# Scan runs of a four-layer kernel: four of the 64 products by C of each run go to VectorE, and the products with D's diagonal are set one by one

## The reference

```python
def step(hst, inp):
    dt_t, B_t, C_t, x_t = inp
    dA = jnp.exp(dt_t[:, :, None] * A)
    hst = hst * dA + (dt_t * x_t)[:, :, None] * B_t[:, None, :]
    y = jnp.einsum('bds,bs->bd', hst, C_t)
    return (hst, y)
...
y = jnp.transpose(ys, (1, 0, 2)) + xm * D_param
```

## Time and profile before

| what | us |
|---|---|
| median of 3 runs | 1950.43 (1948.98 to 1952.22) |
| span of the profiled execution, first to last instruction | 1947.4 |
| what lies around the span (1950.43 less 1947.4; the page gives no time of its own for the profiled execution) | 3.0 |
| the six runs from their first scan to their last, together | 938.0 |
| TensorE busy over the span | 1845.8 (95%) |
| VectorE, ScalarE, GpSimd busy | 1602.8, 1424.0, 1049.0 |

### The profile page before, as it was taken

How to read it: one execution, slowest core, us unless ns; L and a number is a source line. 1 busy time by engine, 2 the same in 40 slices (tenths; PEclk the granted TensorE clock), 3 DMA queues, 4 the chain that set the end, 5 groups by cost and what they waited for, 6 DMA issues and landing times.

```text
span 1947.4 us, 32682 instructions
## 1 busy us (share of the span) xinstructions
PE 1845.8 (95%) x12312; PEld 1335.2 (69%) x12312; DVE 1602.8 (82%) x2125; ACT 1424.0 (73%) x2661; POOL 1049.0 (54%) x603
## 2 busy tenths in 40 slices
PE   6989899998999999999999999999998999999997
PEld 3664899848998599969995899689974333332323
DVE  5565799678998699989995999889977999999742
ACT  3426899468993899799974999799954377777775
POOL 3031599526994299939980699479944400003000
PEclk9989899998999999999999999999998799999999
DMA  5022111111111112101110111021101111111000
GB/s 202 1 85 99 61 55 61 44 64 33 56 60 37 52 51 60 51 24 55 56 44 2 44 55 56 24 75 57 56 15 33 37 42 37 37 36 36 18 23 22
DMA packets 57547, 95.18 MB, mean 49 GB/s; under 512 B 14951, under 2 KB 23559, under 8 KB 55982
## 3 DMA queue, kind: packets, MB, share of 16 engines
q1 hardware_dynamic: 55854, 88.90, 14.9%
q0 software_dynamic: 1536, 4.20, 0.7%
HBM read 73.55 MB, written 6.91 MB: 41 GB/s over the span
## 4 chain that ended last, share of the span: by engine, by line
PE 66%; POOL 9%; ACT 9%; DVE 8%; issue 6%; DMA 1%; SPq 1%; DVEq 0%; ACTq 0%; POOLq 0%
PE PS L865 12%; PE PS L840 11%; POOL A L1019 8%; PE PS L256 7%; PE PS L1603 6%; PE PS L1556 6%; PE PS L846 5%; PE PS L1763 5%; PE PS L265 3%; DVE A L1569 2%; PE PS L872 2%; ACT A L931 2%; PE PS L441 2%; ACT A L908 1%; DVE ST L206 1%
## 5 line engine op out<-in xcount | busy, mean ns | idle before, releaser
L1019 POOL TENSOR_TENSOR A<-A 128x1024 f32<-128x1024 f32 x384 | 897.7, 2392 | 228.7 <-ACT small L923 104.4
L931 ACT ACTIVATE A<-A,negA 128x512 f32<-128x512 f32 x768 | 546.7, 714 | 30.8 <-DVE A L1000 24.1
L1000 DVE TENSOR_TENSOR_SCAN A<-A,PS 128x512 f32<-128x512 f32 x384 | 435.8, 1200 | 46.6 <-PE PS L846 24.1
L1000 DVE TENSOR_TENSOR_SCAN A<-A,small,PS 128x512 f32<-128x512 f32 x384 | 453.9, 1258 | 8.0 <-ACT A L931 5.0
L865 PE MATMUL PS<-ident,A 128*128 128x128 f32 x3072 | 409.1, 276 | 21.5 <-ACT A L737 13.1
L840 PE MATMUL PS<-A 128*128 128x128 f32 x3072 | 384.2, 276 | 1.5 <-ACT A L915 1.2
L865 PEld LDWEIGHTS PS<-ident,A 128*128 128x128 f32 x3072 | 352.9, 143 | 31.2 <-ACT A L737 15.6
L840 PEld LDWEIGHTS PS<-A 128*128 128x128 f32 x3072 | 363.2, 192 | 4.3 <-DVE A L1000 2.8
L1569 DVE TENSOR_REDUCE A<-PS 128x1 f32<-128x512 f32 x512 | 319.5, 681 | 40.2 <-PE PS L1556 38.7
L1800 ACT ACTIVATE A<-PS 128x512 f32<-128x512 f32 x512 | 267.4, 602 | 102.1 <-PE PS L1763 101.9
L908 ACT ACTIVATE A<-A,small 128x512 f32<-128x512 f32 x320 | 228.3, 714 | 21.7 <-PE PS L846 21.3
(11 more groups left out here) (194 smaller groups left out, 1802.5 us busy)
## 6 DMA issues: line engine op xcount, KB each, us to landing
A<-scrc SPq DMA_DIRECT2D x192, 256.0 KB, 3.1
A<-A SPq DMA_DIRECT2D x360, 32.0 KB
scr<-A SPq DMA_DIRECT2D x4, 1024.0 KB, 4.8
W<-in_wa SPq DMA_DIRECT2D x2, 1536.0 KB, 9.7
X<-in_x SPq DMA_DIRECT2D x4, 512.0 KB, 5.5
scr<-W SPq DMA_DIRECT2D x128, 1.5 KB
out<-X SPq DMA_DIRECT2D x4, 512.0 KB, 2.9
W<-in_w SPq DMA_DIRECT2D x1, 1984.0 KB, 7.7
```

The costliest lines, as they stand in the source:

```text
L931: e.activation(A_B[i % 4], r.DT[:, dt, ci * 512:(ci + 1) * 512], ACT.Exp, scale=negA[:, r.n, dt * 16 + s:dt * 16 + s + 1]).then_inc(*decay ...
L1000: e.tensor_tensor_scan(h, a, u, init, ALU.mult, ALU.add).then_inc(*scanned.up((q, i)))
L1019: e.tensor_tensor(h, h, CB[k % 2].unsqueeze(1).broadcast_to([128, 2, 512]), ALU.mult).then_inc(*weighed.up((q, pair)))
```

## The change

Three things change. Pairs 15, 31, 47 and 63 are multiplied by C's row on VectorE instead of GpSimd, each behind the scans of the next pair (before the scan of unit 34, 66 and 98, and behind the last scan), with a semaphore of its own. TensorE, ScalarE and SyncE do what they did, and wait for that semaphore where it is one of these pairs. The products with D's diagonal, four in a row at units 19, 23, 27 and 31 of each half, stand one at a time behind each odd unit from k = 3 to k = 10 of the half.

```diff
+        ON_VECTOR = (15, 31, 47, 63)
+
+        def weighed_at(q, pair):
+            return (weighed_v if pair in ON_VECTOR else weighed).at((q, pair))
...
                 if k >= 2:
-                    w.wait_ge(*weighed.at((q, 2 * (k - 2) + 1)))
+                    w.wait_ge(*weighed_at(q, 2 * (k - 2)))
+                    w.wait_ge(*weighed_at(q, 2 * (k - 2) + 1))
...
-                w.wait_ge(*weighed.at((q, pair)))
+                w.wait_ge(*weighed_at(q, pair))
...
-            def add_skip(ci, dt):
+            def add_skip(ci, n):
+                dt, j = divmod(n, 4)
                 w.wait_ge(*dve.at(("diag", q)))
-                for j in range(4):
-                    e.matmul(PS[:, j, dt * 128:(dt + 1) * 128], r.U[:, dt, ci * 512 + j * 128:ci * 512 + (j + 1) * 128], diag[:, dt, :],
-                             start=open_y(ci, j), stop=True, skip_group_check=True)
+                e.matmul(PS[:, j, dt * 128:(dt + 1) * 128], r.U[:, dt, ci * 512 + j * 128:ci * 512 + (j + 1) * 128], diag[:, dt, :],
+                         start=open_y(ci, j), stop=True, skip_group_check=True)
...
-                if dt == 3 and 4 <= s < 8:
-                    add_skip(ci, s - 4)
+                if 3 <= s < 11 and dt % 2:
+                    add_skip(ci, 2 * (s - 3) + dt // 2)
...
+            def weigh(pair):
+                k = pair // 2
+                w.wait_ge(*scanned.at((q, 2 * pair + 1)))
+                if r.steps[k][0] == r.order[0]:
+                    w.wait_ge(*carried.at((q, pair)))
+                w.wait_ge(*transfer(f"c_load{k % 2}").at((q, k)))
+                h = r.H[pair % HS]
+                e.tensor_tensor(h, h, CB[k % 2].unsqueeze(1).broadcast_to([128, 2, 512]), ALU.mult).then_inc(*weighed_v.up((q, pair)))
+
             for i in range(UNITS):
                 k, dt = divmod(i, 4)
                 ci, s = r.steps[k]
+                if i % 2 == 0 and i // 2 - 2 in ON_VECTOR:
+                    weigh(i // 2 - 2)
...
+            weigh(PAIRS_N - 1)
...
             for pair in range(PAIRS_N):
+                if pair in ON_VECTOR:
+                    continue
```

More of the change, by code:

```diff
@@ L159, in program @@
         decayed, scanned, carried = sig("decayed"), sig("scanned"), sig("carried")
-        weighed, added = sig("weighed_by_c"), sig("added_up")
+        weighed, weighed_v, added = sig("weighed_by_c"), sig("weighed_by_c_on_vector"), sig("added_up")
         taken = sig("y_taken")
```

## The result

The changed kernel took 1956.36 us (median of 7 runs, 1953.58 to 1961.40), the kernel before 1950.43 (1948.29 to 1952.22): ratio 1.0029, 95% interval 1.0017 to 1.0041. Slower, by 5.9 us between the medians: a small difference, 0.3%, but the interval lies wholly above 1. The forecast was slower, 1957.8 us.

The account below looks back on a forecast made before the run. TensorE was taken to bound each run until scan 72, then VectorE's queue, GpSimd 0.2 us behind. Terms 1.4 + 3.0 + 3.0 = 7.4 us gave 1954.8, plus 3.0 (median above span) 1957.8; own range 1954 to 1962, wider 1946 to 1970.

Parts of the forecast that it names:

- What bounds the kernel: In each run: TensorE's queue sets scan 72, VectorE's own queue sets the end from there, GpSimd 0.2 us late.
- D's products, taken 0 for scan 72: First half: spreading them shrinks VectorE's waits, but TensorE has the same records, so scan 72 doesn't move; 0 us.
- Products 15 and 31: Before scan 72: 1.14 us each, covered by VectorE's idle time in runs 0, 1, 2, 4; 31 costs +1.14 in runs 3, 5.
- The extra 0.6 us a run: At product 31: if GpSimd is no earlier, VectorE waits 0.6 us for pair 30, 3.6 over six runs.
- Product 47: After scan 72: +1.14 us in each run, less 0.8 of recovered waits for TensorE, net +0.34.
- Pair 62 late by 0.95 us: End of a run: GpSimd's product ends 0.95 us behind the last scan, not 0.2; +0.75 in four runs, 3.0 in all.
- Waiting products: Rival at 31 and 47: VectorE's products wait for GpSimd's, 1.93 us each, 23 us and 1981, or 1972; chance 0.15.
- Idle time goes: Rival: VectorE's idle 4.2 us a run goes and 3.4 comes, -4.6 us in all, 1945.8; chance 0.13.
- Nearly all covered: Rival: all 1.1 us of waiting comes back and pair 62 isn't late, 2.5 us, 1952.9; chance 0.20.

Follow-up runs that it names:

- e10: Kernel before with D's products of the first half left out and those of the second spread, no product by C on VectorE; ratio to before 0.9902.
- e2: Kernel before with only D's products spread in both halves, all products by C on GpSimd; ratio to before 0.9975.
- e3: Changed kernel with product 47 given back to GpSimd, 15, 31 and 63 staying on VectorE; ratio to before 0.9998.
- e4: Changed kernel with two more products, 39 and 55, on VectorE, six in all; ratio to before 1.0089.
- e7: Changed kernel with only product 47 on VectorE, D's products spread in both halves; ratio to before 1.0009.
- e13: Kernel before with D's products spread in the second half alone, no product by C on VectorE, nothing left out; ratio to before 1.0016.
- e1: Changed kernel with D's products in groups as before, products 15, 31, 47 and 63 still on VectorE; ratio to before 1.0040.
- e5: Changed kernel with VectorE's products 15, 31 and 47 set one scan later; ratio to before 1.0095.
- e12: As e10, D's products of the first half left out, but with products 15 and 63 on VectorE; ratio to before 0.9919.
- e11: Changed kernel with D's products of the first half left out, 15, 31, 47 and 63 on VectorE; ratio to before 0.9960.
- e8: Changed kernel with only product 31 on VectorE, D's products spread in both halves; ratio to before 0.9992.

## Why the prediction was right, and where it wasn't

**What bounds the kernel.** TensorE until scan 72: right, by e10 and by the scan 72 that e2 leaves unmoved. VectorE from there: right, by the 1.13 us per product in e3, e4 and e7. That GpSimd stands 0.2 us beside it: right (pair 62 ends 0.12 to 0.30 us behind the last scan), and more important than I made it (e13).

**D's products, taken 0 for scan 72.** Right: from scan 14 to scan 72 of run 0 69.68 us before, after and in e2. That the place of these records in the first half earns nothing was too narrow; it sets when GpSimd can start its catching up, and how much pause is left behind product 15.

**Products 15 and 31.** Covered in runs 0, 1 and 2, as said (in run 4 scan 72 came 0.24 us later, with the slower start of that run: its first 14 scans took 18.1 us instead of 16.8); in runs 3 and 5 scan 72 came 1.04 us later behind scan 14, for a reckoned 1.14. The cover was reckoned too simply: the idle 2.57 us of the stretch were counted wherever they lay, and most of them lay ahead of product 15. It held because the spread moved them (e1 shows the case without). The extra 0.6 us a run that I named for a GpSimd no earlier didn't come with the change (the 24 products take 1.19 to 1.32 us); it shows in e1, where product 31 takes 0.44 us more in run 0.

**Product 47.** 1.14 less 0.8, +0.34; seen: from scan 14 to the end of the last scan +0.18, +0.18, +0.19 and +0.42 us in runs 0, 1, 2, 4. The recovered waits were 0.96, not 0.8. Runs 3 and 5, reckoned +1.5: +1.55 and +1.30, 0.26 of the former in a second half at a granted clock of 0.98. This half of the sum was reckoned at 4.4 us and is 3.8 by the trace.

**Pair 62 late by 0.95 us, 3.0 us in all: wrong.** It ends 0.10 to 0.12 us behind the last scan, and the gating begins 0.15 us sooner behind it in runs 0 and 1, at the same distance in 3 and 5. The failing step is "GpSimd starts about 1.1 us late. At 2.33 against 2.34 it doesn't make that up". I put VectorE's product into GpSimd's queue as a delay, and not into the scans that GpSimd runs after: they are later by the same 1.14 us. The rows of pair 48 and 49 show both, 3.26 us and then a wait of 0.22 for VectorE.

**The sum.** By the trace the stretches with the changed instructions cost 3.5 us, not 7.4. The measured 5.7 has 2.2 more. All three lie inside the interval of 3.3 to 8.0, so the measured time alone doesn't tell them apart; the rest of the changed kernel's span is 6.5 us longer than before's, and a part of the 2.2 may lie there. That 1957.8 came within 1.5 us of 1956.36 owes something to luck: a term of 3.0 that isn't there stands beside about 2 us that the moved instructions don't explain.

**The rivals.** Waiting products: hardly with the change (at most 0.12 us, product 31 of run 1), but one scan later they cost 12.9 us, and without the spread a first part of it is seen. Idle time goes: VectorE's idle time between scan 14 and pair 31 did shrink, 2.57 to 1.41 us, and only because products filled it; refuted by e2, which leaves scan 72 in place. Nearly all covered: its 2.5 us was nearer to the traced 3.5 than the forecast's 7.4 was; of its two reasons one was right, that pair 62 isn't late, and the other nearly, 0.96 of the 1.1 us of waiting came back. So the mechanism by the traces is this rival's rather than the forecast's, though the measured 5.7 is nearer to 7.4 than to 2.5.

The better version is the spread with all products on GpSimd (e2), 1945.0 us, or with 15 and 63 moved (e6), 1944.9: both faster than the kernel before and the changed one (ratios 0.9975 and 0.9972). They don't differ measurably.

## What to carry to other kernels

Where three engines are busy for the same time, cut a run at the places where another engine begins to set the pace, and price an edit in each piece by the rule of that piece: here the same product cost nothing before scan 72 in the runs where TensorE set the pace there, and 1.13 us behind it. When an inserted instruction delays a producer, the consumer's deadline moves with it. Before moving work between VectorE and GpSimd with both operands in SBUF, see where the other one stands at that moment; a relief can turn into a wait for the very work that is left (e5, e12).

## What was not expected of the hardware

Stretches without any changed instruction differ between the profiled executions. The first scan starts between 202.6 us (e1) and 209.0 (e7, e12), and from the last scan of run 5 to the end it takes 521.6 us (e1) to 526.0 (e13). The window from 80 to 130 us, of before and then of the changed kernel, columns as above:

```profile
80.00:130.00 50.00, 48.39 (x349) 44.12 (x348) 32.41 (x117) 17.18 (x30) 4.92 (x3) 0.97 0.17 61
```

```profile
80.00:130.00 50.00, 48.28 (x320) 43.43 (x319) 29.20 (x109) 17.31 (x30) 4.92 (x3) 0.90 0.12 42
```

TensorE is busy for the same 48 us and gets through 349 or 320 records, with a mean granted clock of 0.97 or 0.90, a mixture of its levels of 2.4 and 1.2 GHz; in the 80 us ahead of it it had been busy for 62.1 and 61.7 us. In before, e4, e5, e6, e10 and e11 the first scan starts at 205.2 to 205.5 us, at a clock of 0.97 in this window (e1 too, 202.6); in the others at 208.2 to 209.0, at 0.90 or 0.93. The same at the start of a run: the first 14 scans of run 2 take 18.17 us in before at a granted clock of 0.91, and 16.78 in e1 at 1.00. And inside a run: in run 3 of e8 the way from scan 72 to the last is 1.1 us longer than in its other runs, with 0.97 in a window where they have 1.00. One profile per kernel doesn't show whether this goes with a kernel or an execution. The table gives a hint: where the rest is far from before's (the changed kernel, e1, e3, e13, e10), the measured time of all executions is off the traced one with the same sign, which chance in single executions would hardly do five times. The profiles do show that a difference of 3 us between two spans here can't be read as the change's, and it is why the table counts from scan 14.
